# A windowed-attention and top-2 mixture block on one core: the written order of the last two units, three PSUM banks for their mixing, and an output tile of its own

## The reference

```
x = x + window_attention(layernorm_over_channels(x))   # x: (16, 56, 56, 32), windows 7x7, shift 3, 4 heads
t = tokens(x)                                           # 16 x 3136 tokens of 32 channels
probs = softmax(layernorm(t) @ router_w + router_b)     # 8 experts
top_p, top_i = top_k(probs, 2);  top_p = top_p / sum(top_p)
expert_out = einsum("bnd,edc->bnec", layernorm(t), expert_w) + expert_b
t = t + sum over the two experts of top_p * expert_out[top_i]
```

## Time and profile before

| | us |
|---|---|
| median of 3 runs | 881.97 |
| the three runs | 894.95, 881.97, 878.93 |
| the profiled execution, own time | 878.54 |
| its span | 876.7 |
| TensorE matmul busy | 691.1 (79%) |
| VectorE busy | 545.8 (62%) |
| GpSimd busy | 484.6 (55%) |
| ScalarE busy | 390.6 (45%) |

### The profile page before, as it was taken

How to read it: one execution, slowest core, us unless ns; L and a number is a source line. 1 busy time by engine, 2 the same in 40 slices (tenths; PEclk the granted TensorE clock), 3 DMA queues, 4 the chain that set the end, 5 groups by cost and what they waited for, 6 DMA issues and landing times.

```text
span 876.7 us, 29477 instructions
## 1 busy us (share of the span) xinstructions
PE 691.1 (79%) x12610; PEld 450.1 (51%) x12640; DVE 545.8 (62%) x1005; ACT 390.6 (45%) x705; POOL 484.6 (55%) x539
## 2 busy tenths in 40 slices
PE   0677879979897979898988989897979898876334
PEld 0355555646565555655555646655565556542201
DVE  7333656768685767666766758676766676744232
ACT  1635454636364545445563636464645555220000
POOL 4345675575757575756665474667675653520310
PEclk9969988999998999999998889999999999955555
DMA  4000221413232322213231323232321313030120
GB/s 121 19 3 3 57 57 39 88 45 76 58 76 57 66 58 58 67 38 76 55 78 39 76 57 76 57 67 59 74 57 41 76 30 76 17 79 0 43 49 18
DMA packets 19009, 47.90 MB, mean 55 GB/s; under 512 B 9536, under 2 KB 9664, under 8 KB 17344
## 3 DMA queue, kind: packets, MB, share of 16 engines
q1 hardware_dynamic: 18448, 45.06, 22.1%
q10 hardware_dynamic: 432, 0.97, 0.3%
HBM read 7.47 MB, written 6.42 MB: 16 GB/s over the span
## 4 chain that ended last, share of the span: by engine, by line
PE 53%; DVE 24%; issue 11%; ACT 5%; POOL 4%; SPq 2%; DMA 0%; DVEq 0%; ACTq 0%; POOLq 0%
DVE mx L851 8%; PE ps_acc L1273 7%; PE ps_weight L1256 7%; PE ps_win L1176 6%; PE ps_shared L1102 6%; PE ps_win L1147 5%; PE ps_pv L1191 4%; DVE zt L966 4%; PE ps_shared L1129 4%; PE ps_shared L1113 3%; PE ps_shared L1213 3%; PE ps_acc L1268 2%; PE ps_win L1170 2%; DVE x L892 2%; DVE ms L865 2%
## 5 line engine op out<-in xcount | busy, mean ns | idle before, releaser
L851 DVE TENSOR_REDUCE mx<-ps_win 128x32 f32<-128x1568 f32 x64 | 114.5, 1789 | 69.9 <-PE ps_win L1147 69.4
L966 DVE TENSOR_TENSOR zt<-ps_weight,x 128x392 f32<-128x392 f32 x128 | 71.8, 561 | 105.8 <-PE ps_weight L1256 105.3
L1256 PE MATMUL ps_weight<-wt,const_bf_tile 96*128 96x392 bf16 x256 | 95.5, 373 | 45.2 <-DVE zt L966 30.0
L761 ACT ACTIVATE pt<-ps_win 128x784 f32<-128x784 f32 x128 | 98.5, 821 | 43.7 <-PE ps_win L1176 43.2
L596 POOL TENSOR_TENSOR on<-on,obs 128x256 f32<-128x256 f32 x64 | 46.7, 729 | 118.9 <-DVE on L878 94.2
L1191 PEld LDWEIGHTS ps_pv<-vb,pt 128*49 128x49 f32 x4096 | 103.7, 127 | 14.6 <-issue 12.4
L966 DVE TENSOR_TENSOR x<-ps_weight,x 128x392 f32<-128x392 f32 x128 | 72.3, 565 | 60.2 <-PE ps_weight L1256 59.3
L1191 PE MATMUL ps_pv<-vb,pt 128*49 128x18 f32 x4096 | 108.6, 200 | 0.0
L1256 PEld LDWEIGHTS ps_weight<-wt,const_bf_tile 96*128 96x128 bf16 x256 | 25.7, 100 | 103.6 <-DVE zt L966 57.7
L751 ACT COPY mr<-ps_win 128x512 bf16<-128x512 bf16 x64 | 37.4, 585 | 92.5 <-PE ps_win L1155 92.5
L575 POOL TENSOR_TENSOR st<-st,minus_half 112x28 f32<-112x28 f32 x16 | 77.1, 4821 | 1.3
(11 more groups left out here) (129 smaller groups left out, 1315.3 us busy)
## 6 DMA issues: line engine op xcount, KB each, us to landing
x<-x SPq DMA_DIRECT2D x48, 392.0 KB, 5.1
x_kept<-xin SPq DMA_DIRECT2D x16, 392.0 KB, 3.4
x<-x2t SPq DMA_DIRECT2D x64, 98.0 KB, 2.2
xin<-x SPq DMA_DIRECT2D x32, 150.0 KB
out<-x SPq DMA_DIRECT2D x32, 150.0 KB
xin<-x SPq DMA_DIRECT2D x32, 18.0 KB
out<-x SPq DMA_DIRECT2D x32, 18.0 KB
xin<-x SPq DMA_DIRECT2D x32, 15.6 KB
```

The costliest lines, as they stand in the source:

```text
L761: nc.scalar.activation(pt[g % 2][:, k, :, :, :].rearrange("p a h n -> p a (h n)"), ps_win[:, :, HN * k:HN * k + HN], ACT.Exp).then_inc(pro ...
L851: nc.vector.tensor_reduce(mx[g % 2].rearrange("n a x h -> n a (x h)"), ps_win[:, :, 0:8 * N].rearrange("n a (k m) -> n a k m", m=N), AX, A ...
L966: nc.vector.tensor_tensor(tokens if eh else zt[:, a, :], ps_weight[:, 0:HALF], tokens, ALU.mult).then_inc(weight_drained, 1)
L1256: mm(ps_weight[:, 0:HALF], weight_sel[:, eh, a, :], wt[:, HALF * half:HALF * half + HALF], start=True, stop=True).then_inc(weight_filled, 1)
```

## The change

`TAIL` is written anew. The order is now: ot 1, wt(14), y 0, back 0, y 1, back 1, norm2_center, norm2_square, mix(14) 0, norm2_scale, mix 1 to 9, mix_drain 0, mix 10, x2t 0 and 1, mix 11, replicate, mix 12, router, mix 13, top2 0 to 2, mix 14, top2_exp, mix 15 and 16, top2 3 and 4, mix_drain 1, final(14), store(14), wt(15), mix(15) 0, top2 5, mix 1 to 5, top2 6, mix 6 to 9, mix_drain 0, top2 7, mix 10 to 16, mix_drain 1, final(15), store(15). The fills of the late part of units 14 and 15 go in turn to `ps_weight` and two banks of `ps_win`, and a fill waits for the one three before it; `wt` of these units waits for the last exponentials of unit 15, which read `ps_win`. The second halves of `y` and `x2t` of unit 15 go to a fourth bank. `final` of every unit writes to the new tile `xo`, and the store reads that.

```
-TAIL = ((1, 1), (0, 3), (1, 1), (0, 1), (1, 1), (0, 2), (1, 1), (0, 1), (1, 1), (0, 5), (1, 1), (0, 6), (1, 1),
-        (0, 5), (1, 4), (0, 1), (1, 8), (2, 24))
+TAIL = ((1, 1), (0, 1), (1, 6), (0, 1), (1, 1), (0, 11), (1, 2), (0, 1), (1, 1), (0, 1), (1, 1), (0, 1), (1, 3), (0, 1), (1, 1), (0, 2), (1, 2), (0, 4), (2, 2), (1, 1), (2, 5), (1, 1), (2, 5), (1, 1), (2, 12))
...
+        xo = sb("xo", [ROWS, A, WS, C])
...
+        def weight_bank(w, fill):
+
+            spare = w.number is not None and w.number >= UNITS - 2
+            return (ps_weight, ps_win[:, 1, :], ps_win[:, 2, :])[fill % 3 if spare else 0]
+
+        def weight_free(w, fill):
+
+            return fill - 3 if w.number is not None and w.number >= UNITS - 2 else fill - 1
+
+        def token_bank(w, fill):
+
+            spare = w.number == UNITS - 1 and fill in (1, 3)
+            return ps_win[:, 3, :] if spare else ps_shared
...
             def store(w, _):
                 sp.wait_ge(weight_drained, upto("weight_drained", w))
-                for tile, dram in pieces(out, x2[w.par], w):
+                for tile, dram in pieces(out, xo, w):
...
             def residual(w, i):
...
                     if w.has_before(2):
-                        dve.wait_ge(out_stored, upto("out_stored", w.before(2)))
+                        dve.wait_ge(weight_drained, upto("weight_drained", w.before(2)))
...
             def final(w, i):
                 dve.wait_ge(weight_filled, upto("weight_filled", w, 17 + i))
                 k0, k1 = (0, 4) if i == 0 else (4, 7)
+                if i == 0 and w.has_before(1):
+                    dve.wait_ge(out_stored, upto("out_stored", w.before(1)))
...
             def wt_turn(w, _):
                 if w.has_before(1):
                     pe.wait_ge(weight_drained, upto("weight_drained", w.before(1)))
+                if w.number is not None and w.number >= UNITS - 2:
+                    pe.wait_ge(probs_ready, UNITS * per_unit["probs_ready"])
...
-                    pe.wait_ge(weight_drained, upto("weight_drained", w, i))
-                    mm(ps_weight[:, 0:HALF], weight_sel[:, eh, a, :], wt[:, HALF * half:HALF * half + HALF],
+                    pe.wait_ge(weight_drained, upto("weight_drained", w, max(0, weight_free(w, 1 + i))))
+                    mm(weight_bank(w, 1 + i)[:, 0:HALF], weight_sel[:, eh, a, :], wt[:, HALF * half:HALF * half + HALF],
                             start=True, stop=True).then_inc(weight_filled, 1)
...
             def final(w, i):
                 pe.wait_ge(sum_drained, upto("sum_drained", w))
-                pe.wait_ge(weight_drained, upto("weight_drained", w, 16 + i))
-                turn_back(ps_weight, i).then_inc(weight_filled, 1)
+                pe.wait_ge(weight_drained, upto("weight_drained", w, weight_free(w, 17 + i)))
+                turn_back(weight_bank(w, 17 + i), i).then_inc(weight_filled, 1)
```

More of the change, by code:

```diff
@@ L769, in x2t_drain @@
                 c0, c1 = (0, 4 * ROWS) if i == 0 else (4 * ROWS, COLS)
-                nc.scalar.copy(x2t[:, c0:c1], ps_shared[:, 0:c1 - c0]).then_inc(token_drained, 1)
+                nc.scalar.copy(x2t[:, c0:c1], token_bank(w, 2 + i)[:, 0:c1 - c0]).then_inc(token_drained, 1)
             def top2_exp(w, _):
@@ L890, in residual @@
                     if w.has_before(2):
-                        dve.wait_ge(out_stored, upto("out_stored", w.before(2)))
+                        dve.wait_ge(weight_drained, upto("weight_drained", w.before(2)))
                 nc.vector.tensor_tensor(
                     x2[w.par][:, :, k0:k1, :].rearrange("p j k c -> p k j c"),
-                    ps_shared[0:ROWS, 0:(k1 - k0) * 128].rearrange("p (k j c) -> p k j c", j=A, c=C),
+                    token_bank(w, i)[0:ROWS, 0:(k1 - k0) * 128].rearrange("p (k j c) -> p k j c", j=A, c=C),
                     x_kept[w.par][:, :, k0:k1, :].rearrange("p j k c -> p k j c"), ALU.add).then_inc(token_drained, 1)
@@ L965, in mix @@
                 tokens = x4[w.par][:, a, HALF * half:HALF * half + HALF]
-                nc.vector.tensor_tensor(tokens if eh else zt[:, a, :], ps_weight[:, 0:HALF], tokens,
+                nc.vector.tensor_tensor(tokens if eh else zt[:, a, :], weight_bank(w, 1 + i)[:, 0:HALF], tokens,
                                         ALU.mult).then_inc(weight_drained, 1)
@@ L971, in final @@
                 k0, k1 = (0, 4) if i == 0 else (4, 7)
+                if i == 0 and w.has_before(1):
+                    dve.wait_ge(out_stored, upto("out_stored", w.before(1)))
                 tokens = x2[w.par][:, :, k0:k1, :].rearrange("p j k c -> p k j c")
                 nc.vector.tensor_tensor(
-                    tokens, ps_weight[0:ROWS, 0:(k1 - k0) * 128].rearrange("p (k j c) -> p k j c", j=A, c=C),
+                    xo[:, :, k0:k1, :].rearrange("p j k c -> p k j c"), weight_bank(w, 17 + i)[0:ROWS, 0:(k1 - k0) * 128].rearrange("p (k j c) -> p k j c", j=A, c=C),
                     tokens, ALU.add).then_inc(weight_drained, 1)
@@ L1079, in shared_free, with token_free @@
                         return
+            def token_free(name, w, i):
+                if token_bank(w, (0 if name == "y" else 2) + i) is ps_shared:
+                    shared_free(name, w, i)
+                else:
+                    pe.wait_ge(probs_ready, upto("probs_ready", w))
             def pre_free(v, i, fill):
@@ L1205, in y @@
             def y(w, i):
-                shared_free("y", w, i)
+                token_free("y", w, i)
+                bank = token_bank(w, i)
                 pe.wait_ge(ot_drained, upto("ot_drained", w))
                 k0, k1 = (0, 4) if i == 0 else (4, 7)
-                mm(ps_shared[0:ROWS, 0:128 * (k1 - k0)], first3[:, 0:ROWS],
+                mm(bank[0:ROWS, 0:128 * (k1 - k0)], first3[:, 0:ROWS],
                    bp.rearrange("p q c -> p (q c)")[:, 0:128 * (k1 - k0)], start=True, stop=False, skip_group_check=True)
                 for k in range(k0, k1):
-                    ins = mm(ps_shared[0:ROWS, (k % 4) * 128:(k % 4) * 128 + 128], ot[:, k, :], w_proj_rows,
+                    ins = mm(bank[0:ROWS, (k % 4) * 128:(k % 4) * 128 + 128], ot[:, k, :], w_proj_rows,
                              start=False, stop=True, skip_group_check=True)
@@ L1224, in x2t_turn @@
             def x2t_turn(w, i):
-                shared_free("x2t", w, i)
+                token_free("x2t", w, i)
                 pe.wait_ge(normed2, upto("normed2", w))
                 for k in range(*((0, 4) if i == 0 else (4, 7))):
-                    ins = nc.tensor.transpose(ps_shared[:, (k % 4) * ROWS:(k % 4) * ROWS + ROWS],
+                    ins = nc.tensor.transpose(token_bank(w, 2 + i)[:, (k % 4) * ROWS:(k % 4) * ROWS + ROWS],
                                               xc2[:, k, :, :].rearrange("p j c -> p (j c)"), ident[0:ROWS, 0:ROWS])
```

## The result

| | before | after |
|---|---|---|
| median of the timed runs, us | 885.20 (4 runs, 878.93 to 894.95) | 847.75 (4 runs, 841.45 to 850.32) |
| ratio to before | | 0.959, 95% interval 0.950 to 0.968 |
| profiled execution, own time | 878.54 | 841.45 |
| its span | 876.7 | 839.6 |

The forecast was 849 in a range of 841 to 860. The profiled execution of after is the fastest of its four runs, so the profile gives the parts and the runs give the ratio. Medians are over all runs of a kernel; a ratio leaves out, on both sides, the runs that lie over 1.5% above the fastest of their kernel.

What follows compares the result with a forecast made beforehand. It took the tail to be bound by unit 15 alone and one-bank ping-pong in the mixings. Gains 20.6 + 8.1 + 0.8 + 2 = 31.5 gave own time 847.0; 2 added for the median made 849, range 841 to 860.

Steps and rivals of the forecast that it cites:

- Part 1: Norm of unit 15 ahead of unit 14's mixing: unit 15's mixing starts at 822.7 in place of 843.29, gain 20.6 us.
- the walk: Step-by-step count of the tail's new order with durations of before and TensorE at 1.2 GHz throughout; alone it gives 851.
- rival c: Tail: norm2_scale and top2 each hold VectorE's queue some 4 us, 6.2 go to the end: 855. Chance 0.1.
- Part 2: Three banks for unit 15's mixing: 16.1 us from first fill to final turn in place of 24.2, gain 8.1.
- rival (b): Mixing: the banks bring nothing, only the order does, since fills don't run ahead: 857 to 861. Chance 0.12.
- Part 3: Final of unit 15 on two banks: the second turn no longer waits for the first drain, 2.6 us, gain 0.8.
- Part 4: The tile xo in all 16 units: added and removed store waits are over long before, cost taken as nothing.
- The clock: TensorE's granted clock rising in the tail: gain of 0 to 9.8 us, taken as 2 for one short rise.
- rival (a): The clock comes back in most of the tail: 9.8 us in place of 2, time 841. Chance 0.17.
- two rules: TensorE's clock: sustained activity releases the half rate (841), or cycling through PSUM banks with small pauses drops it again (851).
- Rival (d): Final in each of 15 units waits for the previous store to land from xo, making the kernel slower: 900. Chance 0.02.
- Rival (e): Unit 15's replicate DMAs come as late as its mixing began before, so the earlier norm gains nothing: 870. Chance 0.04.

Runs made afterwards that it cites:

- the second profile: The changed kernel run again without any edit, profiled a second time: 55.2 us from wt of unit 14 to the end, median 845.07.
- order only: The changed kernel with one bank for every mixing and without xo, only the tail's new order kept: 80.2 us in the tail, ratio to before 0.993.
- the corners: Four kernels without xo, tail in us: before 92.8, new order on one bank 80.2, three banks in the old order 65.5, both 56.2.
- the run with the earlier mixing: The changed kernel with more of unit 14's mixing ahead of norm2_scale and x2t, no product among top2's steps: ratio to before 0.957, median 844.04.
- keep busy: The changed kernel with added matmuls that nobody reads in TensorE's pauses of the tail: 55.0 us in the tail, median 847.98.

## Why the prediction was right

**What bounds the kernel** held: the stretch of unit 15 alone and the two ping-pongs were what the change could take, and it took 38.8 us of the tail (92.8 to 54.0), 37.6 in the second profile. The loop is what it was, within its spread.

**Part 1** was forecast to have the mixing of unit 15 begin 38.8 us after wt of unit 14; it was 33.3 and 34.7. Against the walk the first profile lacks 2.2 in y and the residuals, 1.4 from norm2 to the router's start, 1.3 in the router and 0.6 from there to the end of top2. y, the turn and the router ran at 2.4 GHz in place of 1.2; 0.5 of the 1.4 is the fill of mix 10, which the walk had ahead of the turn and which was out before norm2 was ready. Sum to norm2, 12.8 against 12.9, and POOL's stretch, 6.7 against 6.8, are as walked, since they have no TensorE in them. That top2 and the norm would hold VectorE and not matter (rival c) held too, with banks; on one bank (order only) a form of it came true in TensorE's queue.

**The attribution failed.** I wrote 20.6 to the order and 8.1 to the banks. The walk of part 1 used the count of part 2 for unit 14, so the 20.6 needed the banks; by the corners the order is worth 9 to 13 and the banks 24 to 27. The sum was right because both were in it. For the same reason rival (b), banks without effect, was priced at 857 to 861; the run with order and xo on one bank has 79.0 in the tail, 25.0 more than after. Its argument, that unit 14 on one bank would be late by up to 4, overlooked that x2t and router stand behind unit 14's mixing in TensorE's queue: the logits come at 29.9 in place of 19.2.

**Part 2**: 16.1 from the first fill to the final turn was forecast, 13.1 measured (818.91 to 832.01). At 1.2 GHz the walk was good where it can be compared: group 1 was to end at 5.15, and by the chain it ended at 823.98, 5.07 after the first fill; group 2 was to end at 8.3, and in the run with the earlier mixing, still at 1.2 GHz there, it ended at 8.2. VectorE's products start 0.48 apart when nothing holds them, where I took 0.60.

**Part 3**: 2.6 forecast, 1.84 measured (832.01 to 833.85), at the higher clock. **Part 4**: nothing of the wait in `final` is seen, but the wait that xo removes is worth 0.9 to 1.2 with the new order where y runs at the lower clock, which the sum had in it without my saying so.

**The clock** is the term that was mis-sized: 2 taken, 0 to 9.8 as bounds. The walk at 1.2 GHz has 63.3 from wt of unit 14 to the end, the two profiles have 9.3 and 8.1 less. Of the 9.3, 0.5 is the fill of mix 10 and 0.6 lies in top2's stretch; the other 8.2 lie in y, the turn, the router, the mixing and the final turn, which ran in whole or in part at the higher clock. So the profile looks like rival (a), and the profiled execution, at 841.45, like its number; the other three runs are at 847 to 850, and what separates them from it was not profiled.

The weighing of the two rules of the page "TensorE: Matmul & The Clock Gate" of the Trainium skill (What's actually happening; A second HAM failure mode) comes out between them: the clock does come back in the mixing with three banks, as sustained activity would have it, but 15 us with TensorE shown busy throughout stayed at 0.50.

**The number** was nearer than the working deserved. For the profiled execution the sum said 847.0, and it took 841.45, 5.5 less: 7.3 less in the tail, most of it by the clock that was mis-sized, and 1.7 more ahead of it. For the distance of the median from the profiled execution I added 2, and it was 6.3. The two errors have opposite signs, and what is left of them is the 1.25 between 849 and 847.75: that is luck.

**Rival (d)** had no trace: in after no L989 waits for a DMA. **Rival (e)**: the replicate DMAs were not waited for.

## What to carry to other kernels

An order that puts a second chain beside a first one shares the engines' queues with it: count what stands ahead of each moved step, with the speed that the first chain will then have, and run the corners before crediting the parts. A step moved earlier meets waits that used to be over; the store of two units back, invisible before, was worth about 1 us here. Where executions of the same code differ by more than the part in question, measure from a fixed event ahead of the changed stretch, and compare two profiles only where their steps had the same clock.

## What the runs showed of the hardware

- The granted clock of TensorE was 0.50 over 15 us in which the windows show it busy for 5.0 of 5 us each, matmuls of bf16 and fp32 and transposes mixed (keep busy, 804 to 819). In another execution it was at 1.00 in 801 to 806, with 3.96 of 5 busy. In the mixing of unit 15 it rose 5 to 10 us after the first fill in eight profiles of eight with three banks, not at all with two, and after more than 14 us with two and the pauses filled (13.57 of 13.94 busy until then). What raises it stays open.
- VectorE instructions of 0.56 us that depend on nothing new start 0.48 apart (820.41 and 820.89): the recorded duration is longer than the spacing.
